# A fused layer on Trainium2: raw weight blocks land in the slots of their low parts, vb22 and vt1 are evicted ahead of casts of weights, and GpSimd makes the sums of six blocks

## The reference

```python
def cond(x, y, weight):                      # x (2, 2048, 512)
    ys = y / sqrt(512)
    d = rsqrt(einsum('bi,io->bo', ys * ys, weight * weight) + 1e-8)
    return einsum('bsi,io->bso', x * ys[:, None, :], weight) * d[:, None, :]

def ffn(x, ...):
    xf = x.reshape(-1, 512)                  # 4096 tokens
    top1 = argmax(softmax(xf @ gate_w.T))    # 2 experts
    h = relu(einsum('end,edh->enh', masked, w1) + b1)
    routing_output = (einsum('enh,ehd->end', h, w2) + b2).sum(axis=0)
    shared = relu(xf @ sw1 + sb1) @ sw2 + sb2   # 512 -> 2048 -> 512
    return routing_output + shared

out = x + ffn(cond(x, cond_1024, weight), ...)
```

## Time and profile before

| | |
|---|---|
| time, median of 3 runs | 1482.31 us (1480.47 to 1483.01) |
| the profiled execution's own time | 1482.09 us |
| its span | 1480.1 us, 17706 instructions |
| TensorE busy | 1431.3 us (97%), 6262 matmuls |
| VectorE busy | 848.4 us (57%) |
| ScalarE busy | 501.1 us (34%) |
| GpSimd busy | 314.2 us (21%) |
| DMA | 215.66 MB, mean 146 GB/s |

### The profile page before, as it was taken

How to read it: one execution, slowest core, us unless ns; L and a number is a source line. 1 busy time by engine, 2 the same in 40 slices (tenths; PEclk the granted TensorE clock), 3 DMA queues, 4 the chain that set the end, 5 groups by cost and what they waited for, 6 DMA issues and landing times.

```text
span 1480.1 us, 17706 instructions
## 1 busy us (share of the span) xinstructions
PE 1431.3 (97%) x6262; PEld 1181.0 (80%) x6262; DVE 848.4 (57%) x1362; ACT 501.1 (34%) x776; POOL 314.2 (21%) x354
## 2 busy tenths in 40 slices
...
GB/s 208 235 163 203 223 186 232 173 251 173 222 207 233 269 291 262 275 261 254 219 198 203 67 70 15 54 31 28 57 4 192 75 51 36 27 51 8 67 21 32
DMA packets 157190, 215.66 MB, mean 146 GB/s; under 512 B 46560, under 2 KB 67552, under 8 KB 157120
## 3 DMA queue, kind: packets, MB, share of 16 engines
...
## 4 chain that ended last, share of the span: by engine, by line
PE 67%; DMA 1%; issue 1%; DVE 1%; POOL 0%; ACT 0%; SPq 0%; POOLq 0%; DVEq 0%; ACTq 0%
PE bank L1973 23%; PE bank L1997 23%; PE bank L1938 20%; DMA hidden_scratch<-vb 1%; DMA hin<-hidden_scratch 1%; PE bank L1993 0%; PE bank L1901 0%; POOL out L770 0%; SPq L567 0%; DVE vt L1331 0%; ACT w_hi L877 0%; DMA out<-res,tab 0%; POOL out L773 0%; DVE res L1728 0%; DVE hl L1316 0%
## 5 line engine op out<-in xcount | busy, mean ns | idle before, releaser
L1901 PE MATMUL bank<-xw,w_hi 128*128 128x512 f32 x896 | 285.9, 401 | 33.9 <-ACT vt L960 33.8
L1938 PE MATMUL bank<-hl,w_hi 128*128 128x512 f32 x896 | 278.2, 392 | 4.3 <-DVE hl L1316 4.3
L1702 DVE CAST h_hi<-hf 128x512 fp32r<-128x512 f32 (+1 forms) x128 | 57.3, 448 | 386.9 <-ACT hf L1076 335.8
L753 POOL DMA_INDIRECT rows_e<-xf_scratch,soft x144 | 142.7, 991 | 638.6 <-DVE xe_lo L1579 250.0
L1076 ACT ACTIVATE hf<-bank,b 128x512 f32<-128x512 f32 (+1 forms) x128 | 87.4, 683 | 547.4 <-PE bank L1973 437.6
L1901 PEld LDWEIGHTS bank<-xw,w_hi 128*128 128x128 f32 x896 | 172.3, 194 | 74.9 <-ACT vt L960 37.2
L1938 PEld LDWEIGHTS bank<-hl,w_hi 128*128 128x128 f32 x896 | 169.4, 189 | 40.5 <-DVE hl L1316 5.1
L1973 PE MATMUL bank<-xe_lo,w_hi 128*128 128x512 f32 (+1 forms) x512 | 197.7, 386 | 0.0
L1973 PE MATMUL bank<-xe_hi,w_hi 128*128 128x512 f32 (+1 forms) x512 | 197.6, 386 | 0.0
L1973 PE MATMUL bank<-xe_hi,w_lo 128*128 128x512 f32 (+1 forms) x512 | 196.0, 386 | 0.0
L1997 PE MATMUL bank<-w_lo,h_hi 128*128 128x512 f32 x496 | 193.0, 389 | 0.0
(11 more groups left out here) (216 smaller groups left out, 1704.2 us busy)
## 6 DMA issues: line engine op xcount, KB each, us to landing
hin<-hidden_scratch SPq DMA_DIRECT2D x112, 512.0 KB
hidden_scratch<-vb SPq DMA_DIRECT2D x80, 512.0 KB, 5.3
hidden_scratch<-vt SPq DMA_DIRECT2D x32, 512.0 KB
stage<-w_pack SPq DMA_DIRECT2D x64, 256.0 KB
ring<-x_cols SPq DMA_DIRECT2D x32, 256.0 KB, 3.7
xf_scratch<-xo SPq DMA_DIRECT2D x32, 256.0 KB, 3.3
raw<-w_shared SPq DMA_DIRECT2D x32, 256.0 KB, 5.1
rows<-xf_scratch SPq DMA_DIRECT2D x16, 512.0 KB
```

The lines of the kernel that those rows point to most:

```text
L753: pool.indirect_dma_start(rows_e[:, c % JN, :], None, xf_dram, bass.IndirectOffsetOnAxis(tab_rows[:, c:c + 1], 0)).then_inc(rows_gathered, ...
L1702: nc.vector.tensor_copy(h_hi[:, buf, 0:filled_n], hf[:, j % 2, 0:filled_n]).then_inc(hh_ready, 4)
L1901: last = nc.tensor.matmul(up_bank(u, UP_BANK[c])[p][:], w[:, DOWN_W[c], pair, part], xw[:, c, x, k, :], start=(c in FRESH and n == 1), sto ...
L1938: last = nc.tensor.matmul(bank[p][:], w[:, DOWN_W[c], i, part], hl[:, n % HL, h, :], start=(i == 0 and q == 0), stop=(i == PAIRS - 1 and q ...
```

## The change

- **Slots.** w8_new is a float32 view over w8_lo. Raw blocks 0 to 7, 12 and 13 land in rows 0 to 3 of their own slot, their sums are made in rows 4 to 6, and the low parts are computed in place. 8 to 11, 14 and 15 keep buffers of their own.
- **Loads.** In the projection blocks 0, 1, 4, 5, 6, 7 are loaded at tiles 3, 6, 14, 16, 20, 23; 2 and 3 at the start of group 0 (their slots lie over memory that the projection uses). At the end of group 12 stand blocks 8 and 9 alone; 10 and 11 at the start of group 13, 14 at that of group 14, 12 and 13 at that of group 15, 15 behind vb11 there.
- **GpSimd** makes the sums of blocks 2 to 7; VectorE keeps the others.
- **ScalarE** takes vb22 and vt1 ahead of the casts of weights and of most x blocks.
- **VectorE** makes the four transposes at the start of the group with g=2, and where two blocks are summed both sums stand ahead of the adds; low parts stand between adds.

```diff
-LOAD_AT = (4, 14, 18)
+LOAD_AT = {3: 0, 6: 1, 14: 4, 16: 5, 20: 6, 23: 7}
...
-RAW_FIRST = {0: (4,), 1: (6,), 12: (8, 9, 10, 11), 14: (12, 13)}
-RAW_SECOND = {0: (3,), 1: (5,), 2: (7,)}
-ROWS_BEFORE = {1: 1, 2: 3}
-ROWS_AFTER = {0: 0, 1: 2}
+RAW_AT_START = {0: (2, 3), 13: (10, 11), 14: (14,), 15: (12, 13)}
+RAW_LATE = {12: (8, 9)}
+ROWS_AT_START = {1: (1, 2)}
+ROWS_LATE = {0: (0,), 1: (3,)}
 RAW_LAST = 2 * PAIRS - 2
-RAW_KB = (208, 184, 188, 192, 196, 160, 164)
-RAW_HOME = (0, 0, 0, 0, 0, 0, 0, 0, 1, 2, 3, 4, 0, 4, 5, 6)
-RAW_USE = tuple(RAW_HOME[:n].count(home) for n, home in enumerate(RAW_HOME))
+RAW_KB = {8: 184, 9: 188, 10: 192, 11: 196, 14: 208, 15: 164}
...
         w8_lo = at(64, "w_lo", [8, PAIRS, 256], F32R)
+        w8_new = at(64, "w_new", [8, PAIRS, 256])
...
+
+            return raws[n][:] if n in raws else w8_new[:, 0:4, n % PAIRS, :]
+
         def sums_of(n):
 
-            return sums if n < 2 * PAIRS - 1 else sums_last
-
-
+            if n < RAW_LAST:
+                return w8_new[:, 4:7, n % PAIRS, :]
...
 
-                home = RAW_HOME[n]
-                if RAW_USE[n]:
-                    before_n = max(m for m in range(n) if RAW_HOME[m] == home)
-                    sp.wait_ge(raw_ready, before_n + 1)
-                    sp.wait_ge(sums_made, 4 * (before_n + 1))
-                if n == PAIRS:
+                if n in (2, 3):
+                    sp.wait_ge(tile_mm, NT)
+                if n in (6, 7):
+                    sp.wait_ge(tile_mm, HALF)
+                if n in (8, 9, 10, 11):
                     sp.wait_ge(xw_lo, STEPS * BLOCKS)
-                if n == PAIRS + 4:
+                if n in (12, 13):
+                    sp.wait_ge(up_mm, PER_GROUP * (GROUPS * BLOCKS - 1))
+                if n == 14:
                     sp.wait_ge(ids_out, NT * DMA)
-                if n >= RAW_LAST:
+                if n == 15:
                     sp.wait_ge(up_mm, PER_GROUP * (GROUPS * BLOCKS - 1) + 10)
                 for h in range(2):
                     src = w_shared[n // PAIRS, n % PAIRS + PAIRS * h].rearrange("p (q n) -> p q n", q=2)
-                    dst = raws[home][:, h:4:2, :] if n < PAIRS else raws[home][:, 2 * h:2 * h + 2, :]
-                    sp.dma_start(dst, src).then_inc(raw_in[home], DMA)
+                    dst = raw_of(n)[:, h:4:2, :] if n < PAIRS else raw_of(n)[:, 2 * h:2 * h + 2, :]
+                    sp.dma_start(dst, src).then_inc(raw_in[n], DMA)
...
-                    sp.wait_ge(raw_ready, in_place + 1)
-                    sp.wait_ge(sums_made, 4 * (in_place + 1))
+                    sp.wait_ge(raw_ready, PAIRS + n + 1)
+                    sp.wait_ge(sums_made, 4 * (PAIRS + n + 1))
                 sp.dma_start(hin[:, n % LOADS, :, :], hidden_units(s, at // PAIRS, at % PAIRS, 2)).then_inc(hin_in[n % LOADS], DMA)
...
                         keep_t3(u - 1)
-                    for n in RAW_SECOND.get(u, ()):
+                    for n in RAW_AT_START.get(u, ()):
                         raw_load(n)
-                    if g in ROWS_BEFORE and s < BLOCKS - 1:
-                        next_rows(s, ROWS_BEFORE[g])
+                    if s < BLOCKS - 1:
+                        for q in ROWS_AT_START.get(g, ()):
+                            next_rows(s, q)
                     if u > 0:
                         keep_t4(u - 1)
                     sp.wait_ge(b11_made, u + 1)
                     keep(vb11[u % 2][:], s, g, 0).then_inc(b11_out[u % 2], DMA)
                     if last:
-                        raw_load(RAW_LAST)
                         raw_load(RAW_LAST + 1)
                     sp.wait_ge(b22_made, u + 1)
                     keep(vb22[:], s, g, 5).then_inc(b22_out, DMA)
-                    if g in ROWS_AFTER and s < BLOCKS - 1:
-                        next_rows(s, ROWS_AFTER[g])
-                    for n in RAW_FIRST.get(u, ()):
+                    if s < BLOCKS - 1:
+                        for q in ROWS_LATE.get(g, ()):
+                            next_rows(s, q)
+                    for n in RAW_LATE.get(u, ()):
                         raw_load(n)
...
+            def raw_sums(n):
+
+                raw, out_n = raw_of(n), sums_of(n)
+                a11, a21, a12, a22 = (raw[:, i, :] for i in range(4))
+                pool.wait_ge(raw_in[n], 2 * DMA)
+                pool.wait_ge(sums_made, 4 * n)
+                nc.gpsimd.tensor_tensor(out_n[:, 1, :], a11, a21, ALU.subtract).then_inc(sums_made, 1)
+                nc.gpsimd.tensor_tensor(a21, a21, a22, ALU.add).then_inc(sums_made, 1)
+                pool.wait_ge(sums_made, 4 * n + 2)
+                nc.gpsimd.tensor_tensor(out_n[:, 0, :], a21, a11, ALU.subtract).then_inc(sums_made, 1)
+                pool.wait_ge(sums_made, 4 * n + 3)
+                nc.gpsimd.tensor_tensor(out_n[:, 2, :], a12, out_n[:, 0, :], ALU.subtract).then_inc(sums_made, 1)
+
+            for n in range(2, PAIRS):
+                raw_sums(n)
             pool.wait_ge(raw_ready, PAIRS)
...
                 take(vb11[u % 2], 0, 0, ACT.Identity)
-                if g == 0:
-                    for i in range(X_EARLY, STEPS):
-                        block_hi(s, i)
                 if more:
                     block_hi(s + 1, 0)
-                for n in jobs[:1]:
-                    raw_hi(n)
                 wait(act, b22_out, DMA * u)
                 wait(act, ht_made, 4 * (u - 1) + 2)
                 take(vb22, 1, 1, ACT.Identity)
-                for n in jobs[:1]:
-                    raw_sums_hi(n)
-                if more:
-                    block_hi(s + 1, 1)
+                if g == 0:
+                    block_hi(s, 5)
                 wait(act, t1_out, DMA * u)
                 take(vt1, 2, 0, ACT.Identity)
                 if more:
+                    block_hi(s + 1, 1)
+                if g == 0:
+                    block_hi(s, 6)
+                for n in jobs[:1]:
+                    raw_hi(n)
+                    raw_sums_hi(n)
+                if more:
                     block_hi(s + 1, 2)
                     block_hi(s + 1, 3)
-                if last:
-                    first_units(0, 2)
                 act.wait_ge(up_added, 6 * u + 2)
                 nc.scalar.activation(vb11[u % 2][:], vb11[u % 2][:], ACT.Relu).then_inc(b11_made, 1)
                 for n in jobs[1:]:
                 if more:
                     block_hi(s + 1, 4)
                 if last:
-                    first_units(2, 4)
+                    first_units(0, 2)
                 act.wait_ge(up_added, 6 * u + 4)
                 nc.scalar.activation(vb22[:], vb22[:], ACT.Relu).then_inc(b22_made, 1)
                 for n in jobs[1:]:
                     raw_sums_hi(n)
                 if last:
-                    first_units(4, 6)
+                    first_units(2, 4)
                 if u == 0:
                     for i in range(RING):
                         act.wait_ge(xf_out[i], DMA * NT // RING)
                 wait(act, t4_out, DMA * u)
                 take(vb21, 6, 1, ACT.Relu)
                 if last:
-                    first_units(6, HL)
+                    first_units(4, HL)
 
             act.wait_ge(tile_mm, NT)
             act.wait_ge(gate_done, NT)
...
                     make_t4(u - 1)
+                if g == 2 and s < BLOCKS - 1:
+                    for i in range(FLIPS):
+                        flip(s + 1, i)
+                if more:
+                    block_lo(s + 1, 0)
+                    x_sum_of(s + 1, 0)
+                    x_sum_of(s + 1, 1)
                 for n in jobs[:1]:
-                    if n > 1:
+                    if n >= PAIRS:
                         raw_sums(n)
                 if g == 0:
-                    for i in range(X_EARLY, STEPS):
-                        block_lo(s, i)
-                for n in jobs[:1]:
-                    raw_lo(n)
-                    raw_sums_lo(n)
+                    block_lo(s, 5)
+                for n in jobs[1:]:
+                    if n >= PAIRS:
+                        raw_sums(n)
                 if u == CHOOSE_GROUP:
                     choose()
                 if u == RANK_GROUP:
                     count()
                 if more:
-                    block_lo(s + 1, 0)
-                    x_sum_of(s + 1, 0)
-                    x_sum_of(s + 1, 1)
                     block_lo(s + 1, 1)
                     x_sum_of(s + 1, 2)
+                if g == 0:
+                    block_lo(s, 6)
                 add(vb11[u % 2], 3, 0, 0)
                 if more:
                     block_lo(s + 1, 2)
                 add(vb11[u % 2], 3, 0, 1)
-                for n in jobs[1:]:
-                    raw_sums(n)
+                for n in jobs[:1]:
+                    raw_lo(n)
                 add(vb22, 4, 2, 0)
-                for n in jobs[1:]:
-                    raw_lo(n)
+                for n in jobs[:1]:
+                    raw_sums_lo(n)
                 add(vb22, 4, 2, 1)
...
```

(3 more changed lines are left out.)

33 lines of the change are left out of this document (20 added, 13 removed).

## The result

The changed kernel takes 1447.95 us (median of 4 runs, 1447.13 to 1448.04), the kernel before beside it 1481.47 us (4 runs): a ratio of 0.977, 95% interval 0.9755 to 0.9789. The forecast was 1452, in a range of 1439 to 1468. The profiled execution took 1448.04 us with a span of 1446.3, 33.8 less than before.

The account below looks back on a forecast made before the run. TensorE was bound by up-stage waits rooted in vb21's DMA landing. From 1482.1: -5.0 projection, -26.7 groups (losses 49.4 to 22.7), +1.0 GpSimd, 0 down stage gave 1451.4, by the median 1451.6: 1452 us, range 1439 to 1468.

Parts of the forecast that it names:

- The root and its chain: Up stage: vb21's late landing holds make_t4, then sums, casts and takes; TensorE waits 33.8 us at c=4.
- Late next is c=6: Up stage: after the reorder, TensorE waits for VectorE's first add into vb22; deadline moves from +10.9 to +16.3.
- the longest cover is put away: Group 3: transposes leave its start, make_t4 at +9.5; stall 4.1, loss 6.1 with the clock, gain only 0.5.
- Group 15: Last up-stage group: make_t4 at +14.6, blocks 12 and 13 landing at 17.2; stall 7.0, loss 9.0 with the clock.
- Groups 4 to 12: Middle up-stage groups: loss 5.5 against 4.1 before, about 1.2 each staying in groups 7 and 11.
- The projection: Raw block 1 in its own slot, loaded at tile 6, ends the wait: gain 5.0 us, bounds 0 to -6.
- GpSimd: Sums of blocks 2 to 7: 1.2 us each (bounds 0.42 to 2.4), hidden, with 1.0 us added for the tail.
- VectorE sheds 24 x 0.35, which buys nothing: Up stage: sums moved to GpSimd save VectorE 0.35 us each, beside the landing, for no gain.
- the landing doesn't come earlier: Rival, chance 0.17: b21's queue place sets make_t4's start, staying 9.5, 12.8, 17.5 in groups 2, 13, 15; total 1467.
- As early as in the quiet groups: Rival, chance 0.13: make_t4 starts near +6.5 also in groups 3 and 13; losses 11, total 1440.
- Ring tiles come late: Rival, chance 0.08: in the projection, loads of blocks 4 and 5 cause a new wait; the 5.0 is lost, total 1457.
- GpSimd didn't decide: Rival, chance 0.04: GpSimd's sums set the end in group 3; at 4.5 us per sum, total 1510.

Follow-up runs that it names:

- e7: Changed kernel with raw blocks 10 and 11 loaded at the end of group 12 behind 8 and 9, as before: 1450.58 us, ratio 0.9776.
- e3: Kernel before with one edit, ScalarE taking vb22 and vt1 ahead of the casts of the first raw block: 1477.78 us, ratio 0.9974.
- e1: Changed kernel with ScalarE's casts of a group's first raw block put back ahead of the takes of vb22 and vt1: 1461.26 us, ratio 0.9866.
- e4: Changed kernel with the four transposes put back to the end of the group with g=2: 1447.95 us, ratio 0.9773.
- e10: Kernel before with raw block 1 alone landing in its own slot, loaded at tile 6 for 14: 1474.96 us, ratio 0.9956.
- e2: Changed kernel with the sums of blocks 2 to 7 on VectorE, none on GpSimd: 1451.49 us, ratio 0.9800.
- e11: Changed kernel with GpSimd's work about doubled, each block's first sum made four times more: 1455.00 us, ratio 0.9822.

## Why the prediction was right, and where not

- **The root and its chain** (vb21's landing, VectorE's make_t4, sums, casts, takes): right. e7 shows the landing, e3 VectorE's order behind it and e1 the casts ahead of the takes.
- **"Late next is c=6":** right. Every wait at c=4 of a microsecond or more but one went, and the two large ones of the five at c=6 have the price that the sum over VectorE's order gave: group 3 4.34 us (forecast 4.1), group 15 6.75 (7.0). The other three are 0.2 to 0.5.
- **Group 3** ("the longest cover is put away"): right, 7.1 for 6.1, so that the group gained nothing (6.6 before). The store of t2 is issued at +4.1 (forecast +4.2), and that of vb21 right behind it lands 5.3 us later. In the kernel before, vb21's store is issued at 176.0 and takes 5.4 us: it landed just as the four transposes ended, so they hid a landing that was as late. e4, with the transposes back, has t2's store at +2.6, make_t4 at +8.6 and a wait of 2.50. The clock took 2.8 us (7.1 - 4.34), not 2.
- **Group 15:** 10.9 for 9.0. The wait at c=6 was right, though block 12 was in at +18.3 and not at +17.2. I had not seen one of 1.09 us at c=4, for vt1's take, just over the 1 us that I had named as a limit, and the clock took 3.1.
- **Groups 4 to 12:** mis-sized, 2.8 for 5.5 (and the terms listed for them add up to 5.7). I let group 11 keep 1.2 (0.1 measured, make_t4 at +5.3 there) and group 4 inherit 1 (0.4).
- **The sum of the groups** came out so near, 22.1 for 22.7, by luck: 3.0 us too little in groups 1, 3 and 15 meet 3.6 too much in groups 4 to 14.
- **The projection:** 5.7 for 5.0, and e10 shows that block 1 is 5.2 of it. The four further loads ahead of ring tiles cost nothing that the trace shows.
- **GpSimd:** the price was right by luck of composition, 1.15 us in the mean of 24 (27.6 us busy), made up of 0.74 alone and up to 1.8 beside VectorE. The +1.0 us for its tail was not there: block 3 was done by 112.0, which is the 118.6 forecast less the 5.7 us by which the up stage came earlier and 0.9 more. Its first sum starts at 103.03, when block 2 is in: no gap of 6 us shows. The 1 to 3 us feared from GpSimd and VectorE blocking each other were not lost either: their instructions did get longer, but groups 0 and 1 lose 0 and 0.1.
- **"VectorE sheds 24 x 0.35, which buys nothing":** wrong. e2 shows that this is worth 3.2 us, in group 2, where my own sum had only 0.5 us over. It failed because I held it against the landing (which comes ahead of the sums' place) and not against c=6 in the one group that had no room.
- **The start of the down stage:** taken as 0, 0.8 better (its first 84 matmuls take 25.9 us for 26.7).
- **The rivals:** "the landing doesn't come earlier" is out in groups 2, 13 and 15 (7.8, 9.3 and 13.9 for 9.5, 12.8 and 17.5), and e7 tests it in group 13. "As early as in the quiet groups" is out too: +9.8 and +9.3 in groups 3 and 13, not 6.5. "Ring tiles come late" is out by the first stretch. GpSimd didn't decide; e11 shows that it starts to at twice its work.

The total is 4 us under the forecast: 0.7 from the projection, 0.6 from the groups, 1.0 from GpSimd's tail, 0.8 from the down stage; and the rest lies between medians and rounding.
